# Experts' gate and up products computed with the weights stationary and the tokens moving, shares multiplied by GpSimd, steps of every engine written in another order

## The reference, cut to what matters

```
logits = h @ router_w.T                       # [tokens, 8]
vals, idx = top_k(softmax(logits), 2); vals /= vals.sum()
combine[t, idx] = vals                        # the shares
for each expert e:
    gate, up = split(h @ gate_up[e].T, 2)     # 176 + 176 columns
    out += combine[:, e:e+1] * ((silu(gate) * up) @ down[e].T)
```

## Time and profile before

| | |
|---|---|
| median of 3 executions | 176.15 us (176.12 to 176.69) |
| the profiled execution | 176.1 us, its span 174.3 us |
| granted TensorE clock, mean | 0.999 |
| busy over the span | PE 162.3 us (93%), PEld 153.5, DVE 122.7 (70%), ACT 88.6 (51%), POOL 51.1 (29%) |

### The profile page before, as it was taken

One profiled execution on the slowest core, in us unless ns is written; L12 is line 12 of the kernel. 1 busy time (PEld: TensorE's weight loads), 2 busy tenths in 40 slices (PEclk: granted clock), 3 DMA queues, 4 the chain that ended last, 5 costly groups with the idle time before them and its releaser, 6 DMA issues. The chain is left out here.

```text
span 174.3 us, 3305 instructions
## 1 busy us (share of the span) xinstructions
PE 162.3 (93%) x1158; PEld 153.5 (88%) x1158; DVE 122.7 (70%) x440; ACT 88.6 (51%) x212; POOL 51.1 (29%) x107
## 2 busy tenths in 40 slices
PE   6999878899888999999999999999999999999980
PEld 6998757879777899998999999999999999999980
DVE  3984888989859888758848785598684566643732
ACT  6310779764742777744226879334664423442510
POOL 4723489895961013001013330003013020020201
PEclk9999999999999999999999999999999999999999
DMA  4999950000000000000010000000100000001000
GB/s 124 273 387 401 357 183 0 0 4 0 0 2 2 0 4 0 0 4 0 0 34 2 0 30 4 0 0 0 36 30 0 0 23 13 0 0 34 27 3 30
DMA packets 6464, 8.74 MB, mean 50 GB/s; under 512 B 560, under 2 KB 6192, under 8 KB 6192
## 3 DMA queue, kind: packets, MB, share of 16 engines
q1 hardware_dynamic: 6448, 8.53, 14.4%
HBM read 7.48 MB, written 1.05 MB: 49 GB/s over the span
## 5 line engine op out<-in xcount | busy, mean ns | idle before, releaser
L288 PE MATMUL ps_gu<-gu_hi,x_hi 128*128 128x352 f32 (+1 forms) x128 | 43.7, 342 | 1.5 <-DVE hid L1540 1.5
L289 PE MATMUL ps_gu<-gu_lo,x_hi 128*128 128x352 f32 (+1 forms) x128 | 41.3, 323 | 0.0
L1540 DVE SCALAR_TENSOR_TENSOR hid<-sil,combine,ps_gu 128x176 f32<-128x176 f32 x64 | 24.1, 391 | 13.6 <-ACT sil L761 12.9
L761 ACT ACTIVATE sil<-ps_gu 128x176 f32<-128x176 f32 x64 | 19.4, 317 | 27.2 <-PE ps_gu L293 27.2
L293 PE MATMUL ps_gu<-gu_hi,x_lo 128*128 128x352 f32 (+1 forms) x128 | 31.1, 324 | 0.1
L288 PEld LDWEIGHTS ps_gu<-gu_hi,x_hi 128*128 128x128 f32 x128 | 24.1, 188 | 2.3 <-issue 1.6
L289 PEld LDWEIGHTS ps_gu<-gu_lo,x_hi 128*128 128x128 f32 x128 | 24.2, 189 | 0.0
L318 PE MATMUL ps_out<-dp_hi,hid_hi 128*128 128x256 f32 x88 | 22.8, 293 | 0.2 <-DVE u_feat L1554 0.2
L293 PEld LDWEIGHTS ps_gu<-gu_hi,x_lo 128*128 128x128 f32 x128 | 22.3, 188 | 0.4 <-DVE x_lo L1493 0.4
L1546 DVE TENSOR_TENSOR hid_lo<-ps_tr,hid_hi 128x512 fp32r<-128x512 f32 (+3 forms) x25 | 15.5, 621 | 10.0 <-ACT hid_hi L767 10.0
L319 PE MATMUL ps_out<-dp_lo,hid_hi 128*128 128x256 f32 x88 | 21.5, 278 | 0.0
(11 more groups left out here) (254 smaller groups left out, 293.6 us busy)
## 6 DMA issues: line engine op xcount, KB each, us to landing
gu_raw<-in_guT SPq DMA_DIRECT2D x1, 2824.0 KB, 12.7
dp_raw<-in_dpT SPq DMA_DIRECT2D x1, 1408.0 KB, 15.9
u_feat<-in_xT SPq DMA_DIRECT2D x4, 256.0 KB, 4.2
w_feat<-in_wT SPq DMA_DIRECT2D x4, 256.0 KB, 10.0
out<-u_feat SPq DMA_DIRECT2D x8, 128.0 KB, 1.7
dw_feat<-in_dwT SPq DMA_DIRECT2D x4, 128.0 KB, 7.4
c_raw<-in_c SPq DMA_DIRECT2D x2, 128.0 KB, 3.5
bt<-in_bT SPq DMA_DIRECT2D x1, 128.0 KB, 2.1
```

The costliest lines, as they stand in the source:

```text
L288: pe.matmul(dst, x2_hi[:, b % 2, c, tok], gu_hi[:, c, col], start=(c == 0), stop=False)
L289: pe.matmul(dst, x2_hi[:, b % 2, c, tok], gu_lo[:, c, col], start=False, stop=False)
L761: act.activation(sil[:, bank_of(b, k)], ps_gu[:, bank_of(b, k), E:E + H], ACT.Silu).then_inc(sil_ready, 1)
L1540: dve.scalar_tensor_tensor(hid[:, t, e * H:(e + 1) * H], sil[:, n], combine[:, t, e:e + 1], ps_gu[:, n, E + H:E + GU], ALU.mult, ALU.mult) ...
```

## The change

What it does, in the order of the prediction:

1. **Gate and up.** The weights become the stationary operand: `gu_hi` and `gu_lo` are laid out as [features, gate or up, 1408 inner columns], and `gate_up(b, p, kind)` makes, for each of the 11 chunks of 128 inner columns, 6 matmuls with 256 tokens moving. Chunks go in pairs p (0 to 5, the last one with a single chunk), kind 0 is gate and kind 1 is up; one call fills a bank of 512 columns with 12 matmuls. The result has the inner columns on the partitions, which is what the down product wants.
2. **No transposes of hid.** `hid_transpose` is gone. `gated(b, p)` (VectorE) multiplies silu(gate) by up into `hid`, `hid_hi_copy` and `hid_lo_sub` read `hid` from SBUF.
3. **Shares.** A token's share now differs along the free dimension. The router has matmuls of its own (`router(b)`: 12 of 8 columns). The shares are transposed (2 small transposes), copied by ScalarE to 8 partitions, written to DRAM (`share_out`, one transfer) and read back, each row repeated over the partitions of its expert (`share_in`, 18 transfers a batch on SyncE's queue, 3, 3, 4, 3, 4 and 1 for the six pairs). GpSimd multiplies (`share_product(b, p)`), 128 by 512. `hid` and `shares` lie in the memory of `gu_raw`, which is free once the weights are split.
4. **Down** runs pair by pair; in batch 3 the two tiles of tokens have banks of their own.
5. **Small ones.** The second scaling of the state space model's output weights goes from GpSimd to ScalarE; the floors in `smooth_ratio` and `act_ratio` are computed in `weight_max` and `weight_max2`, which takes an instruction out of each of the two chains; GpSimd makes `ones` before `ident`.
6. **Order.** All lists are written anew. TensorE has 45 `keep_busy` matmul calls instead of 87. The stores of batch b-1 stand behind `share_in(b)`.

```diff
-            def gate_up(b, k):
-                t, e = SLOT_ORDER[k]
...
-                for c in range(DC):
-                    pe.matmul(dst, x2_hi[:, b % 2, c, tok], gu_hi[:, c, col], start=(c == 0), stop=False)
-                    pe.matmul(dst, x2_hi[:, b % 2, c, tok], gu_lo[:, c, col], start=False, stop=False)
...
+            def router(b):
+                pe.wait_ge(x2lo_ready, halves(b))
...
+                    for c in range(DC):
+                        pe.matmul(dst, x2_hi[:, b % 2, c, tok], router_hi[:, c], start=(c == 0), stop=False)
+                        pe.matmul(dst, x2_hi[:, b % 2, c, tok], router_lo[:, c], start=False, stop=False)
+                        last = pe.matmul(dst, x2_lo[:, b % 2, c, tok], router_hi[:, c], start=False, stop=(c == DC - 1))
...
+            def gate_up(b, p, kind):
+                n = (b * NP + p) * 2 + kind
...
+                if n >= BANKS and kind == 0:
+
+                    pe.wait_ge(act_up_ready, (n - BANKS) // 2 + 1)
+                elif n >= BANKS:
+
+                    pe.wait_ge(sil_ready, (n - BANKS) // 2 + 1)
+                for i, h in enumerate(range(*PAIRS[p])):
+                    dst, col = ps_gu[:, bank_of(b, p, kind), i * S:(i + 1) * S], slice(h * P, (h + 1) * P)
+                    for c in range(DC):
+                        pe.matmul(dst, gu_hi[:, c, kind, col], x2_hi[:, b % 2, c], start=(c == 0), stop=False)
+                        pe.matmul(dst, gu_lo[:, c, kind, col], x2_hi[:, b % 2, c], start=False, stop=False)
...
-            def hid_transpose(b, t, g):
...
-                for c in range(lo, hi):
-                    last = pe.transpose(ps_tr[:, (c - lo) * P:(c - lo + 1) * P], hid[:, t, c * P:(c + 1) * P],
-                                        ident[:])
...
+            def share_out(b):
+                sp.wait_ge(share_ready, b + 1)
+                sp.dma_start(share_rows[b], share_tokens).then_inc(shares_out, 16)
...
+            def share_in(b):
+
+                sp.wait_ge(shares_out, 16 * (b + 1))
...
+                for p in range(NP):
...
+                    for c, lo, hi, e in share_pieces():
+                        if PAIRS[p][0] <= c < PAIRS[p][1]:
+                            sp.dma_start(shares[lo:hi, c], share_rows[b, e:e + 1].broadcast_to([hi - lo, S])).then_inc(
+                                shares_in[p], 16)
...
+            def share_product(b, p):
+                lo, hi = PAIRS[p]
+                pool.wait_ge(act_up_ready, count_of(b, p))
...
+                pool.tensor_tensor(hid[:, lo:hi], hid[:, lo:hi], shares[:, lo:hi], ALU.mult).then_inc(hid_ready, 1)
...
+            def gated(b, p):
+                n, (lo, hi) = b * NP + p, PAIRS[p]
+                dve.wait_ge(sil_ready, n + 1)
+                dve.wait_ge(gu_done, 2 * n + 2)
...
-            def hid_lo_sub(b, t, g):
-                lo, hi = groups(b, t)[g]
...
+            def hid_lo_sub(b, p):
+                lo, hi = PAIRS[p]
+                dve.wait_ge(hid_hi_ready, count_of(b, p))
+                dve.tensor_tensor(hid_lo[:, lo:hi], hid[:, lo:hi], hid_hi[:, lo:hi],
+                                  ALU.subtract).then_inc(hid_lo_ready, 1)
```

More of the change, by code:

```diff
@@ L275, in gate_up, with share_transpose @@
+            def share_transpose(b):
+                pe.wait_ge(route_ready, b + 1)
+                for t in range(TT):
+                    last = pe.transpose(ps_tr[0:E, S + t * P:S + (t + 1) * P], combine[:, t], ident[:])
+                last.then_inc(shareT_done, 1)
+            def gate_up(b, p, kind):
+                n = (b * NP + p) * 2 + kind
+                first = p == 0 and kind == 0
+                if first:
                     pe.wait_ge(x2hi_ready, halves(b))
-                if b == 0 and k == 0:
+                if b == 0:
+                    pe.wait_ge(gul_ready, DC * experts_to(PAIRS[p][1]))
+                if b == 0 and first:
@@ new lines, in gate_up @@
+                for i, h in enumerate(range(*PAIRS[p])):
[3 more added lines that the diff above has]
+                        pe.matmul(dst, gu_lo[:, c, kind, col], x2_hi[:, b % 2, c], start=False, stop=False)
+                    if first and i == 0:
+                        pe.wait_ge(x2lo_ready, halves(b))
+                    for c in range(DC):
+                        last = pe.matmul(dst, gu_hi[:, c, kind, col], x2_lo[:, b % 2, c], start=False,
+                                         stop=(c == DC - 1))
@@ L703, in _ @@
[L703 removed]
+            gate_up(2, 2, 0)
+            gate_up(2, 2, 1)
+            gate_up(2, 3, 0)
+            gate_up(2, 3, 1)
+            down(1, 1, 1)
+            down(1, 1, 2)
+            down(1, 1, 3)
+            down(1, 1, 4)
+            down(1, 1, 5)
+            gate_up(2, 4, 0)
+            x2_transpose(3)
+            gate_up(2, 4, 1)
+            gate_up(2, 5, 0)
+            router(3)
+            gate_up(2, 5, 1)
+            down(2, 0, 0)
+            down(2, 0, 1)
@@ L1687, in _ @@
             state_statistics(3, 1)
+            state_aggregate(3)
+            hid_lo_sub(0, 2)
+            smooth2_a(2)
             quant_scales2(2)
-            state_aggregate(3)
-            hidden(1, 6)
+            hid_lo_sub(0, 3)
+            x_max(3)
+            hid_lo_sub(0, 4)
+            smooth_ratio(3)
+            gated(1, 0)
+            gated(1, 1)
+            smooth_inverse(3)
+            hid_lo_sub(0, 5)
+            weight_max2(3)
+            moe_add(0, 0)
+            quant_scales_w(3)
@@ L1717, in _ @@
+            hid_lo_sub(1, 3)
+            gated(1, 4)
             route_gap(2)
```

1031 lines of the change are left out of this document (469 added, 562 removed).

## The result

The changed kernel takes 168.26 us (median of 4 runs, 168.0 to 168.76), the kernel before 176.13 beside it: a ratio of 0.9555, 95% interval 0.9519 to 0.9591, so 7.2 to 8.5 us less. 167.2 was predicted. The profiled execution took 168.11 us, 166.3 of it the span. It divides like the one before, and of the three fences that follow the first answers to the earlier trace rows and the last to the earlier trace rows.

The account below looks back on a forecast made before the run. The prediction took TensorE's list from 46.64 us on to bound the kernel, between a head and a 4.7 us tail. Its terms, -0.7 - 9.8 + 5.3 + 0.9 - 1.1 - 1.0 - 2.5, sum to -8.9: 167.2 us, range 163 to 171.5.

Parts of the forecast that it names:

- The five terms: TensorE's work: gate and up -0.7, transposes of hid -9.8, router +5.3, share transposes +0.9, moved transposes -1.1 us.
- transposes of hid: TensorE: 88 transposes at 0.11 us go and count in full, -9.8 us.
- router: TensorE: 48 added matmuls of 8 moving columns at 0.11 us each, the price of a transpose, +5.3 us.
- rival 2: Router matmuls at only 0.03 us, 163.4 us, or with the head at its bound of -3.2, 162.7; chance 0.11.
- gate and up: TensorE: 528 matmuls of 256 columns at 0.115 us replace 64 slots, -0.7 us, bounds -1.4 and +0.1.
- The fourth slot's wait: TensorE's 1.38 us wait for the shares, before the fourth gate/up slot, goes: -1.0 us, bounds -1.4 and +2.
- The head: Steps on ScalarE, VectorE and TensorE before the first gate/up matmul get shorter: -2.5 us, bounds -3.2 and +0.5.
- Shares: Shares' transfers, 0.47 us to issue, 1.7 to land: just in time for batch 1's x2, no slack, costing nothing.
- rival 1: Repeated-row share transfers in batch 0 issue or land slower and delay `rstd2(1)` and TensorE: 170 to 173 us; chance 0.14.
- VectorE, GpSimd, tail: Changed work on VectorE, 28 us more products on GpSimd, and the tail after TensorE's last matmuls: nothing each.
- Rival 3: The ring of three banks starves TensorE, whose up calls wait for silu: slower, 178 us at 0.5 us waits; chance 0.07.
- Rival 4: 256-column matmuls with new stationaries cost more, say 0.125 us, and GpSimd's products lengthen against VectorE: 172.5 us; chance 0.06.

Follow-up runs that it names:

- experiment 6: Changed kernel with 32 of 48 router matmuls left out: 168.59 us; separately, the kernel before with 63 of 88 transposes of hid left out: 171.61 us.
- Experiments 1 and 2: The first has its own line; the second rewrote the changed kernel's `one_hot` with three operands, 169.56 us, or reading expert numbers from PSUM, 167.67 us.
- experiment 1: Changed kernel with GpSimd's last two weight remainders starting only after VectorE finished the routing of batch 0: 165.99 us, ratio 0.9412.
- experiment 7's second kernel: experiment 5's kernel with router weights hi and lo side by side, 32 router matmuls in place of 48, one VectorE addition more per batch: 164.40 us.
- experiment 5: experiment 1's kernel with GpSimd's batch 1 statistics ahead of the third share product and x2's normalisations ahead of its hi copy on ScalarE: 165.15 us.

## Why the prediction was right, step by step

**What bounds.** TensorE's list from the first gate/up matmul, as said: 115.27 of 117.86 us busy.

**TensorE's work.** The five terms summed to -5.4, and busy time fell by 5.4. That they agree is partly luck: inside the sum sizes were off and cancelled. With experiment 6's prices:
- transposes of hid: 88 x 0.092 is 8.1, and 19 to 25 groups x 0.09 make 1.7 to 2.2: -9.8 to -10.3, for -9.8 forecast;
- router: 48 x 0.092 = +4.4, not +5.3. The upper end was the right one to take, and the floor of rival 2 is ruled out;
- gate and up: 528 x 0.118 to 0.119 = 62.3 to 62.8 against 61.4, +0.9 to +1.4, not -0.7. This term was mis-sized, beyond its bound of +0.1. "The distance follows the columns in both forms" doesn't hold: 0.16 us for 352 columns scales to 0.1164 for 256, and gate and up took more than that. Half of the price was read from the down product, whose matmuls stand closer.

With +0.7 and -0.9 for the share and the moved transposes (8 and 10 at 0.092) that makes -5.2 to -4.2, and -5.4 was measured. The split by term is worked out, with up to 1.2 us left open; only the router and the transposes were taken away in runs.

**The fourth slot's wait.** This step failed. The forecast was -1.0, from "VectorE has some 8 us of steps", "that is even", and from the claim that the first call to wait on VectorE is the fifth. The wait did go, but waits in all rose by 0.3. The first call to wait is the share transpose ahead of that fifth call, for 2.03 us. The cause was in the prediction's own text, under GpSimd: that it shares SBUF access with VectorE was named and left, because GpSimd's own durations stayed level. The rows looked at were GpSimd's, and in the routing it was VectorE that paid. Experiments 1 and 2 show it. In experiment 1, without it, TensorE has no wait ahead of the fifth call, so the even count would have stood.

**The head.** -2.5 forecast, -2.9 found, and -3.3 to -3.9 in executions whose clock stayed at 1.00 from 8 to 13 us, beyond the bound of -3.2. Of its parts only +1.0 for ScalarE's order was tested, together with a step of VectorE, and taking both back gained nothing. So which parts of the sum hold stays open. That `quant_x(0, 0)` is late may cost nothing while VectorE's half is as late, but this isn't shown.

**Shares.** "Just in time, without slack" holds: x2 of batch 1 cost 0.24 us, then 1.68 as soon as TensorE came 3 us earlier (with one late landing in it), and 6.2 with the transfers doubled. An issue takes 0.48 us (8.72 for 18 in SyncE's queue), as said. The landing took 2.7 to 3.2 us, not 1.7, so rival 1's mechanism was real. TensorE's own 2 us wait ahead of it hid most of its price in the changed kernel, and that is luck for the forecast of nothing.

**VectorE, GpSimd, tail.** Nothing each, as forecast in throughput. Rival 3, the ring of three banks, shows no wait on silu or `gated` anywhere. Rival 4's mechanisms both appeared, small: a product of 512 elements has a mean of 1.40 us in place of 1.28, which made nobody on the path wait, and the 256-column matmul of gate and up is 0.003 to 0.004 dearer than 0.115, where the rival had 0.01. "Priced like `hid_lo_sub` at 0.621" was read from a mean over four shapes: of 512 elements `gated` takes 0.68 us. Off the path this cost nothing either.

**Best version.** The candidate is experiment 7's second kernel: 164.4 us with all three router products, 2.3% below the changed one by the two ratios (0.9336 and 0.9555). Most of that is experiments 1 and 5, two order changes on GpSimd and one on ScalarE; from experiment 5 alone it can't be told.
